# A second layer in software-pipelined slots: fc2's first pair moved behind fc1's fourth block, and four slots in each loop iteration instead of two

## The reference

```python
def _L1_attn_ref(x, omega, wq, wk, wv, wo, bo):      # 16 heads of 64
    q, k, v = _heads(x @ wq.T), _heads(x @ wk.T), _heads(x @ wv.T)
    phi_q, phi_k = _phi(q, omega), _phi(k, omega)    # exp(x @ omega.T - |x|^2 / 2) / 8
    kv_cumsum = jnp.cumsum(jnp.einsum('bhnm,bhnd->bhnmd', phi_k, v), axis=2)
    k_cumsum = jnp.cumsum(phi_k, axis=2)
    out = jnp.einsum('bhnm,bhnmd->bhnd', phi_q, kv_cumsum)
    z = 1.0 / (jnp.einsum('bhnm,bhnm->bhn', phi_q, k_cumsum) + 1e-06)
    return (out * z[..., None]).transpose(0, 2, 1, 3).reshape(b, n, H * D) @ wo.T + bo

def _L1_ffn_ref(x, ln_gamma, ln_beta, fc1_q, fc1_scales, fc1_bias, fc2_q, fc2_scales, fc2_bias):
    h = layernorm(x) * ln_gamma + ln_beta
    y = silu(h @ dequant(fc1_q, fc1_scales) + fc1_bias)        # 256 -> 1024
    return x + 0.5 * (y @ dequant(fc2_q, fc2_scales) + fc2_bias)   # 1024 -> 256
...
h = h + _L1_attn_ref(_layernorm(h), ...)
h = h + _L1_ffn_ref(_layernorm(h), ...)
```

## Time and profile before

| | before |
|---|---|
| median of three runs | 4795.0 us |
| profiled execution, its own time | 4793.58 us |
| its span | 4791.8 us |
| PE busy | 4454.1 us, 93% of the span |
| PEld busy | 3973.3 us, 83% |
| DVE busy | 3397.0 us, 71% |
| ACT busy | 2495.3 us, 52% |
| POOL busy | 1855.2 us, 39% |

### The profile page before, as it was taken

How to read it: one execution, slowest core, us unless ns; L and a number is a source line. 1 busy time by engine, 2 the same in 40 slices (tenths; PEclk the granted TensorE clock), 3 DMA queues, 4 the chain that set the end, 5 groups by cost and what they waited for, 6 DMA issues and landing times.

```text
span 4791.8 us, 120275 instructions
## 1 busy us (share of the span) xinstructions
PE 4454.1 (93%) x43016; PEld 3973.3 (83%) x43016; DVE 3397.0 (71%) x7197; ACT 2495.3 (52%) x5314; POOL 1855.2 (39%) x2018
## 2 busy tenths in 40 slices
PE   3999999999999948999999999999999999999997
PEld 2888888888888847888888888888888888888886
DVE  5899999999999853666666666665666666666665
ACT  2555555555555524555554554554555555555553
POOL 1444444444444422343343343333334333334333
PEclk9999999999999979999999999999999999999998
DMA  2000000000000010000000000000000000000000
GB/s 82 19 23 23 23 23 23 23 23 23 23 23 23 22 41 8 5 15 8 8 11 11 8 8 15 8 8 15 8 8 11 11 8 8 14 8 8 15 5 11
DMA packets 64881, 78.93 MB, mean 16 GB/s; under 512 B 8759, under 2 KB 51127, under 8 KB 64439
## 3 DMA queue, kind: packets, MB, share of 16 engines
q1 hardware_dynamic: 64566, 74.07, 5.4%
HBM read 49.40 MB, written 24.64 MB: 15 GB/s over the span
## 4 chain that ended last, share of the span: by engine, by line
PE 45%; issue 9%; POOL 5%; DVE 2%; ACT 1%; POOLq 0%; DMA 0%; DVEq 0%; ACTq 0%; SPq 0%
PE bA L930 9%; PE bA L931 8%; PE bA L932 8%; PE bS L1216 3%; PE bO L1239 2%; PE bA L1303 2%; PE bB L930 2%; POOL sqs_lo L1636 2%; PE bB L1202 2%; PE bB L932 2%; PE bB L931 2%; PE bB L1203 2%; PE bA L1304 1%; PE bT L1256 1%; POOL yT_lo L1594 1%
## 5 line engine op out<-in xcount | busy, mean ns | idle before, releaser
L1636 POOL TENSOR_TENSOR sqs_lo<-sq,sqs_hi 128x768 fp32r<-128x768 f32 x256 | 471.4, 1842 | 811.7 <-ACT sqs_hi L1356 803.9
L1447 DVE TENSOR_TENSOR qk_lo<-bA,qk_hi 128x384 fp32r<-128x384 f32 x512 | 283.4, 553 | 626.4 <-ACT qk_hi L1356 626.2
L1375 ACT ACTIVATE phi<-bB 128x768 f32<-128x768 f32 x256 | 207.9, 812 | 681.2 <-PE bB L1203 681.2
L1594 POOL TENSOR_TENSOR yT_lo<-tanh_y,yT_hi 128x384 fp32r<-128x384 f32 x256 | 258.2, 1009 | 631.2 <-ACT yT_hi L1356 631.2
L1356 ACT ACTIVATE qk_hi<-bA 128x384 fp32r<-128x384 f32 x512 | 251.2, 491 | 229.6 <-PE bA L932 229.6
L1457 DVE TENSOR_TENSOR aT<-bS,mask 128x1024 f32<-128x1024 f32 x256 | 310.9, 1215 | 1.8 <-PE bS L1221 1.6
L930 PE MATMUL bA<-fc_lo,yT_hi 128*128 128x256 f32 x768 | 231.5, 301 | 60.9 <-POOL yT_lo L1594 34.2
L1365 ACT ACTIVATE sq<-bA 128x384 f32<-128x384 f32 x512 | 250.2, 489 | 61.7 <-DVE qk_lo L1447 61.6
L516 PE MATMUL bank<-down_sb,hqT 128*128 128x256 f32 x1128 | 278.5, 389 | 1.0 <-ACT hqT L598 1.0
L614 ACT ACTIVATE kblk<-gu,kb_masked,rowmask 128x128 f32<-128x128 f32 x752 | 270.7, 462 | 6.3 <-PE gu L540 6.3
L516 PEld LDWEIGHTS bank<-down_sb,hqT 128*128 128x128 f32 x1128 | 204.4, 190 | 52.6 <-issue 32.6
(11 more groups left out here) (243 smaller groups left out, 15025.4 us busy)
## 6 DMA issues: line engine op xcount, KB each, us to landing
xT<-in_x SPq DMA_DIRECT2D x94, 256.0 KB, 2.7
h_scratch<-h SPq DMA_DIRECT2D x188, 64.0 KB, 1.9
hx<-h_scratch SPq DMA_DIRECT2D x32, 256.0 KB, 2.7
out<-res SPq DMA_DIRECT2D x32, 256.0 KB, 2.1
hx<-h_scratch SPq DMA_DIRECT2D x64, 64.0 KB, 2.4
out<-res SPq DMA_DIRECT2D x64, 60.0 KB, 1.8
q<-in_fc_q SPq DMA_DIRECT2D x2, 1024.0 KB, 6.2
wq_sb<-in_wq SPq DMA_DIRECT2D x1, 1024.0 KB, 5.0
```

The source lines that it names most:

```text
L1447: dve.tensor_tensor(dst, src, hi.bitcast(fp32), ALU.subtract).then_inc(S[done], 1)
L1594: pool.tensor_tensor(yT[1][:, f % RING, :], tanh_y[f % 2][:], yT[0][:, f % RING, :].bitcast(fp32), ALU.subtract).then_inc(S["y_lo"], 1)
L1636: pool.tensor_tensor(sqs[1][:], sq[:], sqs[0][:].bitcast(fp32), ALU.subtract).then_inc(S["sq_lo"], 1)
```

## The change

Two edits in layer 1. First, the order of the places: the fourth block of fc1 (f3) moves from (4, 1) to (3, 2), and pair 0 of fc2 from (3, 2) to (4, 1), on every engine that has a part in them. Second, the loop's body holds four slots: slots 3 to 26 are six iterations (five taken branches back, one exit), and slots 27 to 34 are straight code.

```diff
+UNROLL = 4
...
-            last = 3 + (SLOTS - 5) // 2 * 2
+            last = 3 + (SLOTS - 5) // UNROLL * UNROLL
...
-            with nc.Fori(3, last, 2, engines=(eng.engine,), hint_back_edge=True) as s:
-                slot(s, 1)
-                slot(s + 1, 0)
+            with nc.Fori(3, last, UNROLL, engines=(eng.engine,), hint_back_edge=True) as s:
+                for u in range(UNROLL):
+                    slot(s + u, (1 + u) % 2)
...
-            for f, (c, n) in enumerate(((2, 1), (2, 2), (3, 1), (4, 1), (4, 2), (5, 2), (6, 1), (7, 2))):
+            for f, (c, n) in enumerate(((2, 1), (2, 2), (3, 1), (3, 2), (4, 2), (5, 2), (6, 1), (7, 2))):
                 p[c][n] = ("fc1", s - 2, f)
-            p[3][2], p[5][1] = ("fc2", s - 2, 0, par), ("fc2", s - 2, 1, par)
+            p[4][1], p[5][1] = ("fc2", s - 2, 0, par), ("fc2", s - 2, 1, par)
```

## The result

The changed kernel takes 4736.38 us (median of four runs, 4733.94 to 4737.43), the kernel before 4792.17 us beside it. The ratio is 0.9881, with a 95% interval from 0.9864 to 0.9898: 1.2% less time, or 55.8 us. The forecast was 4744 us, 50.8 us less than the 4795 us that stood for the kernel before. The profiled execution took 4733.94 us.

A forecast was written before the change was run, and what follows sets the result against it. PE was taken to bound layer 1, so only its idle or slow time could be won. Loop 37.5, places 12.3 and feed-forward-only slots 1 make 50.8 us less: 4744 us, range 4712 to 4775 us.

The forecast's parts named there:

- Part 1: Layer 1's loop: twelve taken branches become five; seven fall away at 5.35 us each, 37.5 us less.
- the sign: Steps between xn transposes on PE: about 95 us only before slots 7, 11, 15, 19 and 23.
- The likeliest case's own range: Whole kernel: 4730 to 4768 us, with the branch price between its bounds and the places' gain between 0 and 14 us.
- Part 2: Places in chunks 3 and 4: a 1.67 us stall becomes 1.54 us; 0.41 us less a slot, 12.3 us over 30 slots.
- the 1 us I had set: The two slots with feed-forward alone: 1 us less, between nothing and one 1.67 us wait.
- Rival 1: At (3, 2) f3 finds its bank free and the stall goes: 4698 us, slots near 87.5 us; chance 0.12.
- Rival 2: In chunk 4, y of f3 is blocked by sqs_lo, f4's block waits about 0.9 us: 4771 us; chance 0.07.
- Rival 3: Layer 1's five remaining branches get dearer as DVE and ACT pay too: 4761 us without cover; chance 0.09.
- Rival 4: New waits at (3, 2) bring the clock to 1.2 GHz, losing 3.4 us a slot: up to 4846 us; chance 0.04.

The follow-up runs named there:

- e2_unroll: Kernel before with four slots in a loop iteration instead of two and the old places: 4748.14 us, ratio 0.9912.
- second profiles: The kernel before and the changed kernel, each profiled once more without an edit: 4792.62 us and 4737.79 us, one run each.
- e3_pre_first: Changed kernel with ACT's pre of f2 ahead of its yT_hi of f1 at place (3, 1): 4710.04 us, ratio 0.9835.
- e7_no_sqs: Changed kernel with POOL's sqs_lo of chunk 3 cut from 384 to 2 columns a row, output not the reference's: 4697.49 us, ratio 0.9803.
- e8_best: Changed kernel with straight code, ACT's pre of f2 before yT_hi of f1, and DVE's y of f1 after attT_lo and its pre of f2: 4676.18 us.
- e1_places: Kernel before with the new places only, still two slots in a loop iteration: 4775.69 us, ratio 0.9971.
- e9_old_head0: Kernel before with only PE's loop head moved to the first slot of an instruction fetch block: 4758.75 us, ratio 0.9944.
- e5_straight: Changed kernel with no loop in layer 1, slots 3 to 34 all straight code: 4717.62 us, ratio 0.9848.

## Why the prediction was right

**What bounds the kernel.** Right: what was won was PE's idle time and lost clock; the instructions of a slot are the same.

**Part 1.** I had seven branches at 5.35 us, 37.5 us. The price was real: a straight program has none of it, and no stretch of half clock between slots 4 and 28 either. By the first profiles, branches and exit together went from 65.5 us (12 x 5.35 + 1.33) to 17.4 us (5 x 3.31 + 0.80), 48 us; by the second profiles from 63.0 to 19.4 us, 44 us; and e2_unroll's own time gives 41 us. The term was 4 to 11 us too small, because I let the five that remain keep the old price. They fell to 3.3 to 3.7 us, so the long steps were 91.9 to 92.9 us in the first profile and not the 95 us that I had named as the sign. Over the two profiles of each kernel the idle time fell by 0.6 us a branch and the lost clock by 1.0 us. The idle time fell because PE's first packet starts earlier; the clock with it, but one profile differs much from the next (1.8 us by the first pair, 0.2 us by the second). The likeliest case's own range was also added up wrongly: its bounds give 4732 to 4771 us, not 4730 to 4768; nothing hangs on it.

**Part 2.** The mechanism was as forecast, to the names: no wait before fc2, 1.05 us (forecast 1.16) before f3, ended by ACT's `pre`, and 0.26 us (0.38) before its second half. The last is smaller because the second half of a block starts 0.46 us behind the first, not 0.35. Chunks 3 and 4 came out within 0.05 us each. These two differences, and 0.08 us more in chunk 5 (11.85 against 11.77 us), make the gain 0.25 us a slot instead of 0.41: 7.5 us in 30 slots, not 12.3. At the end of the layer more was won than the 1 us I had set: behind slot 28 the trace is 6.1 us shorter, of which 1.3 us are the exit and 0.75 us three slots at 0.25 us, so about 4 us belong to the slots that drain the pipeline. By the second profiles it is 6.3 us with an exit of 3.07 us, which leaves 2.5 us. What made them shorter is not shown.

**The sum.** It came nearer than its terms did: part 1 was 4 to 11 us too small, the end of the layer 1.5 to 3 us, and the slots' part of the places 5 us too large. That these offset each other is luck; the mechanism of each is not.

**The rivals.** Rival 1, a stall that goes, did not happen; e3_pre_first and e7_no_sqs, which did make it go, show what was in its way, and that its price was somewhat too high: slots of 88.3 and 88.0 us, and 87.7 us in e8_best, where I had named 87.5. Rival 2 did not happen: y of f3 starts 0.36 us before `sqs_lo` and takes 0.55 us, as f5's does in the earlier trace rows:

```profile
2181.49 0.55 DVE L1523 SCALAR_TENSOR_TENSOR tanh_y<-tanh_y,pre 128x384 f32<-128x384 f32 x1
...
2181.85 1.90 POOL L1637 TENSOR_TENSOR sqs_lo<-sq,sqs_hi 128x768 fp32r<-128x768 f32 x1 [1.02 <-ACT sqs_hi L1357]
```

Rival 3 happened in its mechanism and not in its price. DVE's and ACT's branch instructions stay near 0.07 and 0.05 us, but the instruction behind them comes 0.27 and 0.21 us later than with two slots, and 2.9 and 2.7 us behind the branch without the hint. In the loop of the kernel before, queue 14 carries no instruction packet; in the changed kernel it carries 14 of 8 KB in each iteration. The rule in the Trainium skill's Runtime: NRT & Kernel Launch, § Instruction fetch mechanics, that I had set against the change, a fetch for a taken branch whose target is not there, agrees with that. The hint makes most of it go, and PE's own wait covers the rest, since ACT and DVE wait for PE next. Rival 4 went the other way: the mean granted clock between slots 4 and 28 rose from 0.988 to 0.999.

**What stays open.** Why the first packet starts as late as 1.2 us behind PE's branch in the kernel before (and 0.6 us behind it at two of twelve branches of e1_places), but ahead of it at every branch of the four-slot kernels with a hint and of e9_old_head0. e9_old_head0 shows that it is not the length of the body; only one other place of the head was tried. What brings the clock down is open too. Half clock directly behind a branch was found most often where PE had stood idle longest: at five of five branches with 3.7 us of idle time on average, at eight and nine of twelve with 3.2 us, and at one of twelve and one of five with 1.8 and 1.7 us. But this is not strict: e7_no_sqs had 3.0 us and none.

## What to carry to other kernels

Take a wait that ends on one semaphore as the last of a queue of waits: before a piece is moved there, work out when the next condition of the new piece comes true, which here turned 1.67 us into 1.3 us and left the cause, an instruction order on ACT and DVE, for two small edits worth 41 us together (e5_straight against e8_best). The price of a loop can be read from the steps of a mark that comes once in each slot, with and without a branch between, and the idle time behind the branch is only a part of it, as the clock can fall after it. Whether an engine pays for a branch is read from its next instruction, not from the branch instruction alone, and what it waits for from the instruction packets among the DMA. Where the code may be long, straight code is the simplest cure; where it may not, the place of the loop's head is worth a try.

## What the runs showed of the hardware

- A taken branch of bodies with some 3,600 or 7,300 PE instructions (matmuls and weight loads) stops PE until 1.3 to 1.6 us after a 16 KB instruction packet has landed. The branch instruction takes 1.5 to 2.2 us with a prefetch hint and four slots, 1.5 to 3.6 us with a hint and two, 3.4 to 4.1 us without a hint. Often PE stops once more for 0.3 to 1.5 us, for the next packet; with the head of the loop in the first slot of a fetch block that second wait is gone.
- On ACT and DVE the branch instruction takes 0.04 to 0.08 us in every case. The next instruction comes 0.17 and 0.20 us behind it with two slots, 0.38 and 0.47 us with four, 2.7 and 2.9 us with four and no hint.
- More code costs nothing of itself: 32 slots of straight code, some 1,800 PE instructions each, ran at 89.14 us a slot, with no idle time that a fetch could explain.
- A DVE instruction with two SBUF inputs that starts 0.5 us after a GpSimd one takes 1.7 to 1.8 us instead of 0.55 us; one that starts 0.35 us before it takes 0.55 us.
